# A second layer's loop on one core: the same steps in another order on four engines, and two additions carried into the next unit

## The reference

```python
x = x + jnp.tanh(g_xattn[0]) * _L0_xattn_ref(_layernorm(x), ctx_1024, ctx_1024, ...)
x = x + jnp.tanh(g_ffn[0]) * _L0_ffn_ref(_layernorm(x), W1, b1, W2, b2, Wr, br)
x = x + jnp.tanh(g_xattn[1]) * _L1_xattn_ref(_layernorm(x), ctx_1024, ctx_1024, mask, ...)
x = x + jnp.tanh(g_ffn[1]) * _L1_ffn_ref(_layernorm(x), sim_matrix, gates, q_proj, ...)
```

```python
logits = xn @ sn - jax.nn.sigmoid(gates)          # gate: relu, the two best, softmax -> w
y = jnp.einsum('nc,ech->neh', x, p)               # all 16 experts, for q, k and v
return jnp.einsum('ne,neh->nh', w, y)
attn = softmax(q k^T / sqrt(128)); o = attn v     # inside a sequence
out = jnp.einsum('enh,ehc->nc', jnp.einsum('ne,nh->enh', w, o), o_proj)
```

## Time and profile before

| | us |
|---|---|
| median of 3 runs | 1628.67 (1626.63 to 1629.27) |
| the profiled execution, its own time | 1626.43 |
| its span | 1624.7 |
| TensorE busy in the span | 1513.6 |
| VectorE, GpSimd, ScalarE busy | 1293.3, 1186.9, 1064.2 |

### The profile page before, as it was taken

How to read it: one execution, slowest core, us unless ns; L and a number is a source line. 1 busy time by engine, 2 the same in 40 slices (tenths; PEclk the granted TensorE clock), 3 DMA queues, 4 the chain that set the end, 5 groups by cost and what they waited for, 6 DMA issues and landing times.

```text
span 1624.7 us, 52801 instructions
## 1 busy us (share of the span) xinstructions
PE 1513.6 (93%) x17129; PEld 1308.8 (81%) x17130; DVE 1293.3 (80%) x4044; ACT 1064.2 (65%) x2661; POOL 1186.9 (73%) x1715
## 2 busy tenths in 40 slices
PE   5899999976999789999999999999999999999996
PEld 4666666755999469888888888888888888889885
DVE  3777778863555378998999889988998999988885
ACT  3777777743556456767766776677667766776664
POOL 4556666642456568888888888888888888888785
PEclk9999999986999999999999999999999999999998
DMA  2322222234553100000000000000000000000000
GB/s 78 110 72 74 78 78 78 78 102 120 147 140 91 29 16 15 20 16 15 21 19 17 15 21 15 21 15 21 15 21 15 17 19 21 15 15 18 5 8 11
DMA packets 92108, 69.05 MB, mean 42 GB/s; under 512 B 13937, under 2 KB 87697, under 8 KB 91921
## 3 DMA queue, kind: packets, MB, share of 16 engines
q1 hardware_dynamic: 76512, 49.34, 10.3%
q0 software_dynamic: 5120, 12.62, 2.4%
q10 hardware_dynamic: 10288, 4.74, 1.1%
HBM read 35.74 MB, written 22.52 MB: 36 GB/s over the span
## 4 chain that ended last, share of the span: by engine, by line
PE 79%; issue 7%; DVE 6%; ACT 3%; DMA 2%; POOL 2%; SPq 1%; POOLq 0%; ACTq 0%; DVEq 0%
PE s_bank L1998 12%; PE s_bank L1999 11%; PE s_bank L2000 11%; PE tb L1815 6%; PE po L1945 4%; PE s_bank L1933 4%; PE s_bank L1795 4%; PE po L1829 3%; PE m L1769 2%; PE s_bank L2146 2%; PE s_bank L1804 2%; ACT pT L889 1%; DVE qkv L1552 1%; DMA kx<-kT 1%; PE s_bank L2133 1%
## 5 line engine op out<-in xcount | busy, mean ns | idle before, releaser
L745 POOL TENSOR_TENSOR qkv<-qkv,scaled 128x384 f32<-128x384 f32 x480 | 489.4, 1020 | 87.2 <-ACT scaled L1020 37.8
L1020 ACT ACTIVATE scaled<-s_bank,wg 128x384 f32<-128x384 f32 x449 | 260.3, 584 | 114.5 <-PE s_bank L2000 109.9
L1998 PE MATMUL s_bank<-proj_hi,hn_hi 128*128 128x384 f32 x900 | 327.0, 363 | 5.6 <-DVE qkv L1552 5.6
L1552 DVE SCALAR_TENSOR_TENSOR qkv<-s_bank,wg,qkv 128x384 f32<-128x384 f32 x449 | 273.9, 610 | 49.8 <-PE s_bank L2000 39.6
L1999 PE MATMUL s_bank<-proj_lo,hn_hi 128*128 128x384 f32 x900 | 302.9, 337 | 0.0
L2000 PE MATMUL s_bank<-proj_hi,hn_lo 128*128 128x384 f32 x900 | 302.2, 336 | 0.0
L889 ACT ACTIVATE pT<-tb 128x512 f32<-128x512 f32 x256 | 152.9, 597 | 136.1 <-PE tb L1815 134.5
L1998 PEld LDWEIGHTS s_bank<-proj_hi,hn_hi 128*128 128x128 f32 x900 | 169.4, 188 | 18.9 <-DVE qkv L1552 14.1
L1815 PE MATMUL tb<-ident,prob 128*128 128x128 f32 x1024 | 161.4, 281 | 15.2 <-ACT pT L889 13.8
L1999 PEld LDWEIGHTS s_bank<-proj_lo,hn_hi 128*128 128x128 f32 x900 | 170.2, 189 | 1.6
L2000 PEld LDWEIGHTS s_bank<-proj_hi,hn_lo 128*128 128x128 f32 x900 | 169.0, 188 | 0.0
(11 more groups left out here) (285 smaller groups left out, 3714.3 us busy)
## 6 DMA issues: line engine op xcount, KB each, us to landing
xs<-sorted_in SPq DMA_DIRECT2D x71, 128.5 KB, 2.1
kx<-kT SPq DMA_DIRECT2D x256, 32.0 KB
sorted_out<-yo SPq DMA_DIRECT2D x71, 64.0 KB, 1.6
xin<-in_x SPq DMA_DIRECT2D x32, 128.0 KB, 2.1
cin<-in_ctx SPq DMA_DIRECT2D x32, 128.0 KB, 2.3
ctx_cols<-xcT SPq DMA_DIRECT2D x32, 128.0 KB, 1.7
w<-in_L_ffn_W SPq DMA_DIRECT2D x16, 256.0 KB, 3.8
xcT<-ctx_cols SPq DMA_DIRECT2D x32, 128.0 KB, 2.8
```

Source lines behind the costliest of these rows:

```text
L745: g.tensor_tensor(into, into, scaled[m % SCALED][:, 0:cols], ALU.add).then_inc(dense_added, 1)
L1020: ins = act.activation(into, bank[:, 0:3 * D], ACT.Copy, scale=wg[v % 4][:, 1, k:k + 1])
L1552: v.scalar_tensor_tensor(out=acc, in0=bank[:, 0:3 * D], scalar=wg[w % 4][:, 0, k:k + 1], in1=acc, op0=ALU.mult, op1=ALU.add).then_inc(dens ...
L1998: pe.matmul(bank[:, 0:cols], hi[:, tile], of(proj_hi), start=True, stop=False)
```

## The change

`body1` of TensorE, VectorE, ScalarE and GpSimd get another order; no instruction of a unit is added or dropped, no buffer is changed, and what leads into the loop stays. The head work on TensorE moves forward (`upper_weigh`, `gate_products`), the token work moves back. VectorE's gate steps, until now in four bunches, are spread one or two at a time between the takes. On GpSimd the last two additions of the output parts (`add(u, "o", 2)` and `3`) stand at the head of the next body; so does `residual`, which was between them. Some special cases for u = 0 and u = 1 go. The diff, with the common indent cut:

```diff
@@ -745,27 +745,27 @@
     g.tensor_tensor(into, into, scaled[m % SCALED][:, 0:cols], ALU.add).then_inc(dense_added, 1)
 
 def body1(u):
+if exists(u + 3):
+    residual(1, u + 3, (u + 1) % 2)
+add(u - 1, "o", 2)
+hidden_length(u + 1)
+add(u - 1, "o", 3)
 add(u, "q", 1)
-hidden_length(u + 1)
 gather(u + 4)
-add(u, "q", 2, 3)
-if u == 0:
-    residual(1, 3, 1)
+add(u, "q", 2, 3, 4, 5)
+if exists(u + 4):
+    norm(1, u + 4)
+add(u, "q", 6, 7, 8, 9)
+lower_hidden(u + 1)
+add(u, "q", 10)
+lower_heads(u - 1)
+add(u, "q", 11, 12, 13)
 if u > 0:
     pad_row(u + 3)
-lower_hidden(u + 1)
-add(u, "q", 4, 5, 6, 7, 8, 9, 10)
-lower_heads(u - 1)
-add(u, "q", 11, 12, 13)
-if exists(u + 4):
-    norm(1, u + 4)
-add(u, "q", 14, 15)
+add(u, "q", 14)
+hidden_norm(u + 2)
+add(u, "q", 15)
 add(u, "o", 1)
-hidden_norm(u + 2)
-add(u, "o", 2)
-if exists(u + 4):
-    residual(1, u + 4, u % 2)
-add(u, "o", 3)
 
 pad_row(0)
 g.wait_ge(s[1]["pad_row_ready"], 1)
@@ -1027,41 +1027,42 @@
 
 def body1(u):
 q = s[1]
-take(u, "q", 0)
+if exists(u + 3):
+    copy_xT(u + 3)
 if u == 0:
-    take(u, "q", 1)
-    copy_xT(3)
+    take(u, "q", 0, 1)
 apply_second_norm(1, u + 1, lambda t: x3[(u + 1) % 5][:, t, :], lambda t: hn[:, t, :])
+if u != 0:
+    take(u, "q", 0)
+copy_hidden(u + 1)
 exp_bank(u + 2, 0)
+exp_bank(u + 2, 1)
 if u != 0:
     take(u, "q", 1)
-queries(1, u + 3)
-exp_bank(u + 2, 1)
+keys(1, u + 3)
 exp_bank(u + 2, 2)
 exp_bank(u + 2, 3)
-token_exp(u - 1)
 copy_pT(q, u + 2, 0)
 take(u, "q", 2)
-copy_hidden(u + 1)
-keys(1, u + 3)
-take(u, "q", 3, 4, 5)
 copy_pT(q, u + 2, 1)
+queries(1, u + 3)
+take(u, "q", 3)
 copy_pT(q, u + 2, 2)
+take(u, "q", 4, 5)
+token_exp(u - 1)
 take(u, "q", 6)
+copy_pT(q, u + 2, 3)
+take(u, "q", 7)
+apply_norm(1, u + 4, u % 2)
+take(u, "q", 8)
 token_weights(u - 1)
-take(u, "q", 7, 8)
-copy_pT(q, u + 2, 3)
-take(u, "q", 9)
-copy_v(q, u + 3, (u + 1) % 2)
-take(u, "q", 10, 11)
+take(u, "q", 9, 10, 11, 12)
 token_heads(u - 1)
-take(u, "q", 12)
 gate_exp(u + 1)
 take(u, "q", 13, 14, 15)
 take(u, "o", 0, 1)
-apply_norm(1, u + 4, u % 2)
+copy_v(q, u + 3, (u + 1) % 2)
 take(u, "o", 2, 3)
-copy_xT(u + 4)
 
 q = s[1]
 copy_v(q, 0, 0)
@@ -1596,64 +1597,70 @@
     add_residual(1, 1, 1, x3[1][:, :, :])
     second_rows(1, 1, x3[1])
     second_join(1, 1)
-if u != 1:
-    token_keys(u - 1)
 max_bank(u + 2, 0)
 max_bank(u + 2, 1)
-if u == 1:
-    token_keys(u - 1)
+token_keys(u - 1)
 max_bank(u + 2, 2)
 if u != 0:
     take(u, "q", 1)
 max_bank(u + 2, 3)
 take(u, "q", 2)
-token_max(u - 1)
-take(u, "q", 3, 4)
-total_groups(u - 2)
-result(u - 3)
-token_weights(u - 1)
-take(u, "q", 5)
 if exists(u + 1):
     gate_limit(u + 1, gates)
     gate_inverse(u + 1, gates)
-take(u, "q", 6, 7)
+take(u, "q", 3)
 if exists(u + 1):
     gate_logits(u + 1, gates)
-take(u, "q", 8)
+take(u, "q", 4)
+total_groups(u - 2)
 if exists(u + 1):
     gate_top(u + 1, gates)
-take(u, "q", 9, 10)
+result(u - 3)
 if exists(u + 1):
     gate_index(gates)
+take(u, "q", 5)
+if exists(u + 1):
     gate_floor(gates)
+first_rows(1, u + 4, u % 2)
+take(u, "q", 6)
+token_max(u - 1)
+take(u, "q", 7)
+total(u - 2)
+first_join(1, u + 4)
+take(u, "q", 8)
+token_weights(u - 1)
+take(u, "q", 9)
+if exists(u + 1):
     gate_shift(gates)
     gate_pairs(gates)
-take(u, "q", 11)
-first_rows(1, u + 4, u % 2)
-first_join(1, u + 4)
-take(u, "q", 12)
-total(u - 2)
 turn_heads(q, u + 2)
-invert_sums(q, u + 2)
-divide_heads(q, u + 2)
-return_heads(q, u + 2)
-take(u, "q", 13, 14)
+take(u, "q", 10)
 if exists(u + 1):
     gate_both(gates)
+take(u, "q", 11)
+if exists(u + 1):
     gate_idle(gates)
+invert_sums(q, u + 2)
+take(u, "q", 12)
+if exists(u + 1):
     gate_mask(gates)
-take(u, "q", 15)
-take(u, "o", 0)
+divide_heads(q, u + 2)
+take(u, "q", 13)
+return_heads(q, u + 2)
+take(u, "q", 14, 15)
+if exists(u + 1):
+    gate_select(u + 1, gates, wg[(u + 1) % 4])
+    gate_sum(gates, wg[(u + 1) % 4])
 if exists(u + 2):
     add_residual(1, u + 2, u % 2, x3[(u + 2) % 5][:, :, :])
+take(u, "o", 0)
+second_rows(1, u + 2, x3[(u + 2) % 5])
 take(u, "o", 1)
-second_rows(1, u + 2, x3[(u + 2) % 5])
+if exists(u + 1):
+    gate_divide(gates)
 second_join(1, u + 2)
 take(u, "o", 2, 3)
 if exists(u + 1):
-    gate_select(u + 1, gates, wg[(u + 1) % 4])
-    gate_sum(gates, wg[(u + 1) % 4])
-    gate_divide(gates)
     gate_weights(gates, wg[(u + 1) % 4])
 
 first_rows(1, 0, 0)
@@ -2164,60 +2171,52 @@
 def body1(u):
 if u != 0:
     tokens_parts(u, 0, 0)
-if u != 1:
-    token_transposes(u - 1)
-if u != 0:
     tokens_parts(u, 1, 0)
 upper_scores(u)
-if u == 1:
-    token_transposes(u - 1)
+upper_normed(u + 1)
+token_transposes(u - 1)
+if u != 0:
+    tokens_parts(u, 1, 1)
+subtract_bank(u + 2, 0)
 if u != 0:
     tokens_parts(u, 0, 1)
-    tokens_parts(u, 1, 1)
-subtract_bank(u + 2, 0)
-upper_normed(u + 1)
+gate_products(u + 1)
 upper_queries_keys(u + 3)
 subtract_bank(u + 2, 1)
+tokens_parts(u, 0, 2)
+upper_probs(u + 2, 0)
 subtract_bank(u + 2, 2)
-tokens_parts(u, 0, 2)
-token_scores(u - 1)
+tokens_parts(u, 0, 3)
 subtract_bank(u + 2, 3)
-tokens_parts(u, 0, 3)
-upper_probs(u + 2, 0)
 tokens_parts(u, 0, 4)
 tokens_parts(u, 1, 2)
 tokens_parts(u, 0, 5)
-tokens_parts(u, 1, 3)
+upper_probs(u + 2, 1)
 tokens_parts(u, 0, 6)
-tokens_parts(u, 1, 4)
-gate_products(u + 1)
-upper_probs(u + 2, 1)
-tokens_parts(u, 1, 5)
+tokens_parts(u, 1, 3, 4)
+upper_probs(u + 2, 2)
 tokens_parts(u, 0, 7)
+upper_values(u + 3)
+token_scores(u - 1)
+tokens_parts(u, 1, 5, 6)
+tokens_parts(u, 0, 8)
+upper_probs(u + 2, 3)
+tokens_parts(u, 1, 7)
+tokens_parts(u, 0, 9)
+tokens_parts(u, 1, 8)
+upper_weigh(u + 2)
 token_weights(u - 1)
-tokens_parts(u, 1, 6)
-tokens_parts(u, 0, 8)
-upper_probs(u + 2, 2)
-tokens_parts(u, 0, 9)
-tokens_parts(u, 1, 7)
-tokens_parts(u, 0, 10)
-tokens_parts(u, 1, 8)
-tokens_parts(u, 0, 11)
-tokens_parts(u, 1, 9)
-upper_probs(u + 2, 3)
-tokens_parts(u, 0, 12)
-tokens_parts(u, 1, 10)
-upper_values(u + 3)
-upper_weigh(u + 2)
-tokens_parts(u, 1, 11)
+tokens_parts(u, 0, 10, 11)
+tokens_parts(u, 1, 9, 10)
 token_values(u - 1)
-tokens_parts(u, 1, 12)
-tokens_parts(u, 0, 13, 14)
-tokens_parts(u, 1, 13)
+tokens_parts(u, 0, 12, 13)
+tokens_parts(u, 1, 11, 12)
+tokens_parts(u, 0, 14)
+tokens_parts(u, 1, 13, 14)
+tokens_parts(u, 0, 15)
+outputs_parts(u, 0, 0)
+tokens_parts(u, 1, 15)
 upper_output(u + 2)
-tokens_parts(u, 0, 15)
-tokens_parts(u, 1, 14, 15)
-outputs_parts(u, 0, 0)
 outputs_parts(u, 1, 0)
 outputs_parts(u, 0, 1)
 outputs_parts(u, 1, 1)
```

## The result

The changed kernel took 1640.2 us (median of 20 runs, 1632.2 to 1648.9), the kernel before, on the same chip, 1631.8 us (20 runs, 1624.8 to 1648.2). The ratio is 1.0045, 95% interval 1.0023 to 1.0067: slower by 8.4 us. The forecast was slower by 8.4 us, 1637, range 1614 to 1651. So sign and size came out as forecast, but not for the reason given: the loss is not in the 28 full units, where I had put all of it.

A forecast was written before the change was run, and what follows sets the result against it. TensorE was taken to bound the kernel before, VectorE's cycle of 33.0 us the new one: 28 full units x (33.0 - 32.7) = +8.4, ends zero, 1634.8 on the profiled execution, 1637 us as median; range 1614 to 1651.

The forecast's parts named there:

- The bound of the kernel before: TensorE bounds the loop; 0.39 us of each 32.7 us unit is VectorE's being late, because of GpSimd's additions.
- TensorE's floor: TensorE's shortest unit in the new order, 32.3 us; as rival, 32.3 to 32.5 a unit, 1618 us, chance 0.34.
- joined groups: On TensorE, groups of short matmuls go from 12 to 10 a unit, each costing its successor 0.09: 0.17 us less.
- two new meetings: TensorE meets ScalarE's last take at the masks, and `token_keys` freeing the queries' and keys' bank: 0.1 to 0.2 us together.
- VectorE's cycle: VectorE's work of 31.1 us plus 1.9 of forced waits makes a unit at least 33.0 us, above TensorE's 32.3.
- forced waits: VectorE must wait at least 1.15 us for the scores and 0.7 to 0.8 at `add_residual`, 1.9 together in each unit.
- my lower end of 29.85: VectorE's work in a unit, 30.8 - 0.95 us, if all four newly separated small steps are lucky; upper end 31.65.
- dependent steps with a take between them: On VectorE, such steps no longer wait for each other's end; allowed -0.2 us a unit.
- the wait of a random arrival: A VectorE step standing alone waits 0.45 us on average for one of GpSimd's additions.
- One wait for another: Rival: TensorE's part 7 wait goes, an equal one comes at parts 12 to 14 of tile 0; 1628 us, chance 0.17.
- What would show the forecast wrong: Line 1472 at 181 ns, no VectorE wait listed, 32.3 us units; or ScalarE or GpSimd waits heading the list.
- The ends: In the last units, `token_max` and the exponential come some 1.4 us later, offset by earlier first takes: zero, within 1.5.

The follow-up runs named there:

- short additions: GpSimd adds only 16 columns of each part: old order 1608.6 us against 1626.3, ratio 0.9892; whole new order 1623.3 us, ratio 0.9985.
- the run with the new tail alone: New order from unit 29 on, old order in all units before, against the kernel before: 1632.8 us, ratio 1.0031.

## Why the prediction was right and wrong

**The bound of the kernel before.** Right. TensorE bounds it, VectorE's late take costs 0.39 a unit, and it is late because of GpSimd. The short additions show it directly, and the true sum is a little more, 0.49, with the longer step behind the wait.

**TensorE's floor.** I gave 32.16 for the joined groups, then 32.3 with 0.1 to 0.2 for two new meetings. The joined groups gave more than their 0.17 (three fewer first matmuls, 0.28). The meetings were under-priced, and one was missed: the masks 0.21, output part 0 set apart between token parts 0.30, short groups 0.14. This is the term that made the middle what it is: 32.6 instead of 32.3. I had counted how often short groups interrupt the parts, and had not looked at output part 0, which now comes earlier and finds `lower_heads` late.

**VectorE's cycle.** This is the step that failed. I gave 31.1 of work and 1.9 of forced waits, 33.0 together. The forced waits were right (1.5 + 0.8, and 0.7 for the gather). The work was not: VectorE's waits are now 50.5 us of the stretch of 400 (the four rows of DVE above, and one of 1.3), so a unit of 32.65 holds about 4.1 of waiting and 28.5 of work, gaps included. It fell by over 2 us from the 30.8, under even my lower end of 29.85. With 28.5 of work and the forced waits, VectorE's cycle is hidden behind TensorE.

The larger part of the miss is in the gaps. Added up by line, the durations of VectorE's steps changed by about -0.5 us a unit, where my terms come to +0.5; the other 1.6 are in the gaps between the steps. For these, dependent steps with a take between them, I had allowed 0.2.

The durations themselves moved both ways. Some of the separated steps do wait (duration in ns, min/median/max; the medians before were 747, 192 and 706):

```profile
L1456 DVE TENSOR_SCALAR idle<-top x25: 1078/1232/1377, 652.0 to 1437.7; 128x2 f32<-128x2 f32 x25
L1462 DVE SCALAR_TENSOR_TENSOR lg<-lg,gtop x25: 181/1020/1024, 658.4 to 1444.8; 128x32 f32<-128x32 f32 x25
L1580 DVE TENSOR_TENSOR oall<-halves x25: 415/1127/1245, 655.8 to 1441.6; 128x256 f32<-128x256 f32 x25
```

and `gate_mask` has a median of 529 where it had 192. Others go free: the product with `srs` at 424 ns always, the comparisons at 179 instead of 592, `idle` at 391 instead of 936, `both` at 172. I had charged each separated step with the wait of a random arrival. Most of the steps don't arrive at random: units of the middle are alike within a few hundredths of a us, and the tests and the shift above are long in all but one of 25 units, the product with `srs` short in all. It isn't so for all: the last product of the gate, `gate_weights`, is at 1.0 us in about half the units and at 0.18 in the others. The test `idle<-top` I had also misread: its bare duration is not the 384 ns that is the shortest in the earlier trace rows but 150, as the old order with short additions shows.

**The rivals.** "One wait for another", chance 0.17, is what happened in the middle: the wait at part 7 goes, others of the same size come, the unit stays at 32.6 to 32.8. It named parts 12 to 14 and VectorE; the places are the masks and output part 0, and the second of them waits for GpSimd, behind ScalarE. What would show the forecast wrong included "waits for ScalarE or GpSimd at the head of the list, which I have costed at nothing": that came, with `oh_lo`.

**The ends.** Zero within 1.5 was wrong by far: +2 to 3 (an estimate) and +5. I named the one mechanism, `token_max` behind `total_groups`, at 1.4. The wait at that place grew by 1.9 (4.69 less 2.77), and putting `token_max` back took 0.8 of it. What I left out: that in the last bodies, which have no head work, TensorE waits for the second norm (1.03), the token's weights (0.60 and 0.81) and takes, and that `upper_normed` right behind the scores has no normed rows in the first two units. What I set against the 1.4, an earlier first take in units 30 and 31, is there (waits of 0.61 and 1.07 before the first parts of the kernel before are gone) and doesn't cover these.

**The number.** 8.4 us measured, 8.4 forecast, is luck, a coincidence of two errors: +8.4 for a middle that has 0 in it, and 0 for ends that have 8.

**Left open.** A version that beats both wasn't found. The old order has 0.49 a unit to gain, and only VectorE's take of part 5 hangs on the blocked product; to put the take ahead of `token_weights` was not tried. Nor was the new order with output part 0 joined to the others on TensorE. The tail's 5 us are shown by the run with the new tail alone, but of what makes them up only `token_max` was tried by itself.

## What to carry to other kernels

When one wait is cured by reordering, go through the bounding engine's own list start to start as well, not only through the waits between engines: here the cure was worth 0.49 a unit, and the new order gave 0.39 of it back in pieces of 0.05 to 0.2 us, most of which no list of waits shows. Shorten the suspected cost by itself in both versions before explaining one of them: the two kernels with short additions settled what the list of waits had suggested wrongly. And price the first and last bodies of a deep pipeline on their own, since an order tuned for the full body has no cover there.

## What the runs showed of the hardware

- A VectorE step with two SBUF inputs that meets GpSimd's additions is held for up to 1.5 us more (415 to 1960 ns). The test `idle<-top`, with one tensor input, is held too: 150 ns with short additions, 747 in the kernel before, 1232 in the changed one. For most lines the place alone decides: bare in nearly all of 25 units or blocked in nearly all. Moving one step 0.7 us earlier in the unit made the two behind it wait, and the kernel 34 us slower.
- Short additions (16 columns) leave GpSimd busy 162.6 us of 400 instead of 346 and took 17.7 us from the old order, although GpSimd had only 2% of the chain.
- At full clock the matmul step behind a wait is longer as well: 0.28 us instead of 0.18 behind the wait for VectorE in the kernel before, 0.34 instead of 0.23 at the output part that waits for `oh_lo`. An output part right behind a token part, with nothing to wait for, starts after the usual 0.18.
- The time of an execution goes with TensorE's mean granted clock (0.971 to 0.983, 7 to 8 us for 0.01 in three groups of runs). In the profiled executions of the kernel before and the changed one the second layer is at 1.00 but for two places: the start of its loop (570 to 588), where TensorE has waits of 1 to 2 us, and the last 22 us, where it has waits of 1 to 5 us. For differences of 0.2% the clock has to stand beside the time.
